# Reordering the start of a two-layer FFN kernel: conditioning products inside the first bank, one load issued by ScalarE, one product ahead of a mixing

## Chip, cores and metric

The kernel runs on one NeuronCore of a Trainium2 chip. The metric is the device time of one execution in microseconds (us); lower is better. Three executions of the kernel before gave a median of 1265.41 us (1264.41 to 1265.54).

## What is computed

The input `x` is 64 batches of 64 channels by 1024 values, in f32. Two layers follow each other, each a small conditioned mixing over channels, an expert FFN and a residual addition:

```python
x = x + _L0_ffn_ref(_L0_cond_ref(x, cond_128, ...), weight, lora_A, lora_B, gw1, ..., gw2, gb2)
x = x + _L1_ffn_ref(_L1_cond_ref(x, cond_128, ...), W, b, Wq, Wk, A, Bm)
# _L0_cond_ref: att = softmax(gelu(gelu(cond W0 + b0) W1 + b1) W2 + b2)   (64 x 8)
#               out = (sum_k att_k weight_k) x + att @ bias_k             (64 x 64 mixing per batch)
# _L0_ffn_ref:  out = x W^T + top-2 gated LoRA experts;  _L1_cond_ref: grouped convolution with 9 taps
```

The mixing over channels and the product with the FFN weights commute. The kernel therefore multiplies the unmixed `x` with the weights first, and mixes the result afterwards.

## The kernel before, in words

**Tiles and stages.** The 4096 rows (64 batches x 64 channels) are 32 tiles of 128. Phase A computes the first layer for all tiles and spills its result, phase B computes the second. Every f32 product is made as three products of a high and a low part (`split_product`, L1343 to L1347: hi x hi, hi x lo, lo x hi). So each weight piece and each tile of `x` is first rounded by ScalarE (ACT: `split_hi`, L724; `x_high`, L739), and VectorE (DVE) subtracts to get the low part (`split_lo`, L957; `x_low`, L979).

**Banks.** The first layer has 1184 output columns in three banks (k = 0, 1, 2 of 384, 416 and 384 columns). `main(t, b, k, j0, j1)` (L1409) is tile t's product with bank k over the pieces j0 to j1 of the contraction, 8 in all, three matmuls each. `mix(t, b, k)` (L1429) is the mixing of that bank, three matmuls. Between them ACT rounds the product (`y_high`, L746) and DVE makes its low part (`y_low`, L985). DVE builds the mixing matrix of a tile (`mix_matrix`, L962, about 2.3 us of small operations) and adds the mixed result into a row buffer (`evict`, L991). Tile t's bank 0 mixing writes one PSUM bank for all t, so `mix(2, 2, 0)` waits for `evict(1, 1, 0)`.

**The start.** TensorE (PE) begins with eight throw-away products of 512 columns (`keep_warm`, L1349) and then runs `first_bank` (L1390): tile 0's product with bank 0, piece by piece as the weights arrive, with the column sums of the weights woven in, five matmuls a piece. It needs the second half of tile 0's `x` (pieces 4 to 7) in high and low form for j = 4. The weights of bank 0 come as 8 chunks of 192 KB (n = 0 to 7); chunks 8 to 11 are the halves of banks 1 and 2. `column_sums(k)` (L1379) makes the sums for banks 1 and 2.

**Conditioning.** `cond(0)` to `cond(4)` (L1357) are the small products of the attention over kernels: two hidden layers with a Gelu on ACT after each (L796, L799), the logits, a softmax shared by ACT (L802, after an activation table load at L800) and DVE (L1045 to L1052), a masked product (L1054), then `cond(3)` (L1369), three products whose results give the coefficients `attc` (L1060), and `cond(4)`. No mixing matrix can be built without `attc`.

**Order.** All engines run hand-written orders; semaphores join them. Loads before the change are all issued by SyncE (SP), in program order, on one DMA queue. The orders that matter are SP's at L457 to L487, ACT's at L779 to L826, DVE's at L1025 to L1081 and PE's at L1447 to L1463. Then each engine enters `phase_a(t, b, it)`, whose first call is t = 0, through `periods` (L300). PE's `phase_a` is at L1465, ACT's at L828, DVE's at L1089.

Of the kernel before, what the change touches and what calls it, by code (L numbers as in the profile page):

```python
# [25 lines left out]
P = 128  # L26
# [46 lines left out]
def program(nc, a, out):  # L73
    with ExitStack() as ctx:
# [207 lines left out]
        def half_x(t, h):  # L282

            return xo[:, t, 512 * h:512 * h + 512].rearrange("p (j t) -> p j t", j=4)
# [142 lines left out]
        def _(sp):  # L427
            def chunk(n):
                for m in before[n]:
                    sp.wait_ge(*low_of(m))  # L430
                for src, to, _, _ in parts_of(n):
                    sp.dma_start(to, src).then_inc(stage_in[where[n]], 16)  # L432
# [22 lines left out]
                sp.dma_start(bias_in[:, u, :], src.unsqueeze(0).to_broadcast([P, P])).then_inc(bias_ld[u], 16)  # L455

            sp.dma_start(xo[:, 0, 0:512], a["xt"][0:P, 0:512]).then_inc(first_in, 16)  # L457
            for n in range(4):
                chunk(n)
            sp.dma_start(xo[:, 0, 512:D], a["xt"][0:P, 512:D]).then_inc(xt_in[0], 16)  # L460
            for n in range(4, 8):
                chunk(n)
            sp.dma_start(cbuf[:, 0:CPACK], a["cpack"]).then_inc(cond_in, 16)
            sp.dma_start(xo[:, 1, 0:512], a["xt"][P:2 * P, 0:512]).then_inc(second_in, 16)
# [258 lines left out]
        def _(act):  # L723
# [56 lines left out]
            act.activation(sc[:, 7:8], eps[:, :], ACT.Gelu).then_inc(tables, 1)  # L780
            act.wait_ge(first_in, 16)
            act.activation(x_hl[0][0][:, 0:4, :], half_x(0, 0), ACT.Copy).then_inc(first_hi, 1)
            for n in range(4):
                split_hi(n)
            act.wait_ge(xt_in[0], 16)
            act.activation(x_hl[0][0][:, 4:8, :], half_x(0, 1), ACT.Copy).then_inc(x_hi, 1)
            for n in range(4, 8):
                split_hi(n)
            act.wait_ge(second_in, 16)
            act.activation(x_hl[1][0][:, 0:4, :], half_x(1, 0), ACT.Copy).then_inc(first_hi, 1)  # L790
            act.wait_ge(xt_in[1], 16)
            act.activation(x_hl[1][0][:, 4:8, :], half_x(1, 1), ACT.Copy).then_inc(x_hi, 1)
            y_high(0, 0)
            act.wait_ge(cond_in, 16)
            act.wait_ge(cond_pe, 1)
            act.activation(h1, ps[:, BC[0], 0:B], ACT.Gelu, bias=cb0).then_inc(cond_act, 1)  # L796
            x_high(2, 2, 1)
            act.wait_ge(cond_pe, 2)
            act.activation(h2, ps[:, BC[1], 0:B], ACT.Gelu, bias=cb1).then_inc(cond_act, 1)  # L799
            act.activation(sc[:, 6:7], eps[:, :], ACT.Exp).then_inc(tables, 1)  # L800
            act.wait_ge(cond_dve, 2)
            act.activation(ex, lg, ACT.Exp, bias=am[:, 0:1]).then_inc(cond_act, 1)  # L802
            column_sums(0)
            split_hi(8)
            y_high(1, 0)
            split_hi(9)
            act.wait_ge(cond_pe, 7)
            for h in range(2):
                q = slice(64 * h, 64 * h + 64)
# [18 lines left out]
            def phase_a(t, b, it):  # L828
                if later(t, 2):
                    y_high(t + 2, 0)  # L830
                bias12_of(t + 1)
                if later(t, 1):
                    y_high(t, 1)
                    root(routed(t))
                y_high(t, 2)
                if before_end(t, XB):
                    x_high(t + XB, b, it + 2)
                if at(t, 0):
                    y_high(3, 0)
                    root(1)  # L840
                if before_end(t, AHEAD):
                    bias0_of(t + AHEAD)
                if isinstance(t, int) and t in aside:
                    split_hi(aside[t])
                if at(t, CATCH_UP):
                    root(t + 2)
# [95 lines left out]
        def _(dve):  # L942
# [91 lines left out]
            for n in range(4, 8):  # L1034
# [1 line left out]
            dve.wait_ge(first_hi, 2)  # L1036
            dve.tensor_tensor(x_hl[1][1][:, 0:4, :], half_x(1, 0), f32(x_hl[1][0][:, 0:4, :]),
                              ALU.subtract).then_inc(first_lo, 1)
            dve.wait_ge(x_hi, 2)
            dve.tensor_tensor(x_hl[1][1][:, 4:8, :], half_x(1, 1), f32(x_hl[1][0][:, 4:8, :]),  # L1040
                              ALU.subtract).then_inc(x_lo, 1)
            y_low(0, 0)
            x_low(2, 2)
            dve.wait_ge(cond_pe, 3)
            dve.tensor_tensor(lg, ps[0:B, BC[0], 64:64 + KATT], cb2, ALU.add).then_inc(cond_dve, 1)  # L1045
            dve.wait_ge(cond_dve, 1)
            dve.tensor_reduce(am[:, 0:1], lg, X, ALU.max, negate=True).then_inc(cond_dve, 1)
            dve.wait_ge(cond_act, 3)
            restart(0)
            link(dve.tensor_reduce(am[:, 1:2], ex, X, ALU.add))  # L1050
# [2 lines left out]
            dve.wait_ge(cond_dve, 3)  # L1053
            dve.tensor_tensor(att_m, att[:, None, :].to_broadcast([B, TILES, KATT]),  # L1054
                              batch_tile[:, :, None].to_broadcast([B, TILES, KATT]), ALU.mult).then_inc(cond_dve, 1)
            dve.wait_ge(cond_pe, 5)
            dve.tensor_copy(attT, ps[0:KATT, BC[1], 64:64 + B]).then_inc(cond_dve, 1)
            dve.tensor_tensor(ctxo, ps[0:B, BC[1], 128:128 + C], fs_bc, ALU.add).then_inc(cond_dve, 1)
            dve.wait_ge(cond_pe, 6)
            dve.tensor_copy(attc[:, :, :].rearrange("p t k -> p (t k)"),  # L1060
                            ps[:, BC[0], 128:128 + TILES * KATT]).then_inc(attc_ready, 1)
            split_lo(8)
            split_lo(9)
            dve.wait_ge(zeroed, 4)
            dve.wait_ge(consts_in, 16)
            dve.wait_ge(attc_ready, 1)
            restart(2)
            mix_matrix(0, 0)
            y_low(1, 0)
            split_lo(10)  # L1070
            mix_matrix(1, 1)
# [17 lines left out]
            def phase_a(t, b, it):  # L1089
                u = b % 2  # L1090
                restart(links_before(t))
                if later(t, 2):
                    if at(t, CATCH_UP + 1):
                        y_low(t + 2, 0)
                        evict(t - 1, 1 - u, 2)
                        x_low(t + XB - 1, (b + XB - 1) % XB)
                    else:
                        evict(t - 1, 1 - u, 2)
                        y_low(t + 2, 0)
                if at(t, 0):  # L1100
                    mix_matrix(3, 3)
                    y_low(0, 2)
                    evict(0, 0, 1)
                    evict(2, 0, 0)
                    x_low(4, 0)
                    y_low(3, 0)
                    evict(0, 0, 2)
                    route(1, 1)
                elif at(t, 1):
                    y_low(1, 1)  # L1110
                    route(2, 0)
                    y_low(1, 2)
                    evict(1, 1, 1)
                    evict(3, 1, 0)
                    mix_matrix(4, 0)
                    x_low(5, 1)
                else:
                    mix_matrix(t + AHEAD, (b + AHEAD) % XB)
                    y_low(t, 1)
                    evict(t + 2, u, 0)  # L1120
                    r = routed(t)
                    route(r, r % 2 if isinstance(t, int) else 1 - u)
                    y_low(t, 2)
                    evict(t, u, 1)
                    if at(t, CATCH_UP):
                        route(t + 2, u)
                    elif before_end(t, XB):
                        x_low(t + XB, b)
                assert at(t, CATCH_UP) or links["n"] == A_LINKS + at(t, 0), links["n"]
# [212 lines left out]
        def _(pe):  # L1342
# [47 lines left out]
            def first_bank():  # L1390

                (hi, lo), product, sums = x_hl[0], ps[:, BY0[0], 0:BANK0], ps[:, BM0[0], 0:BANK0]
                for j in range(J):
                    w_hi, w_lo, first, last = w0[0][:, j, 0, :], w0[0][:, j, 1, :], j == 0, j == J - 1
                    if j % 4 == 0:
                        pe.wait_ge(*((first_hi, 1) if first else (x_hi, 1)))
                    pe.wait_ge(stage_hi, j + 1)
                    pe.matmul(product, hi[:, j, :], w_hi, start=first, stop=False, skip_group_check=True)
                    pe.matmul(sums, ones[:, :], w_hi, start=first, stop=False, skip_group_check=True)
                    if j % 4 == 0:  # L1400
                        pe.wait_ge(*((first_lo, 1) if first else (x_lo, 1)))
                    pe.matmul(product, lo[:, j, :], w_hi, start=False, stop=False, skip_group_check=True)
                    pe.wait_ge(*low_of(j))
                    made = pe.matmul(product, hi[:, j, :], w_lo, start=False, stop=last, skip_group_check=True)
                    summed = pe.matmul(sums, ones[:, :], w_lo, start=False, stop=last, skip_group_check=True)
                made.then_inc(main_done[0], 1)
                summed.then_inc(wsum_done, 1)

# [39 lines left out]
            pe.wait_ge(wide_set, 1)  # L1448
            keep_warm(8)
            first_bank()  # L1450
            cond(0)
            main(1, 1, 0, 0, 2)
            cond(1)
            main(1, 1, 0, 2, 4)
            cond(2)
            main(1, 1, 0, 4, 8)
            cond(3)
            main(2, 2, 0, 0, 4)
            cond(4)
            main(2, 2, 0, 4, 8)  # L1460
            column_sums(1)
            pe.wait_ge(zeroed, 4)
            mix(0, 0, 0)  # L1463
# [1 line left out]
            def phase_a(t, b, it):  # L1465
                main(t, b, 1)
                if at(t, 0):
                    mix(1, 1, 0)
                    column_sums(2)
                mix(t + 2, (b + 2) % XB, 0)  # L1470
                main(t, b, 2)
                mix(t, b, 1)
                main(t + AHEAD, (b + AHEAD) % XB, 0)
                mix(t, b, 2)
# [218 lines left out]
```

## Time and profile before

| | before |
|---|---|
| profiled execution | 1265.09 us, span 1263.3 us |
| median of 3 (lowest, highest) | 1265.41 us (1264.41, 1265.54) |
| PE busy | 1257.2 us, 100% of the span, 6967 matmuls |
| DVE busy | 842.7 us, 67% |
| ACT busy | 307.3 us, 24% |
| POOL busy | 235.2 us, 19% |
| chain that ended last | PE 97%, DVE 1%, DMA 1% |

Read the table as follows: the span is what the profiler saw from the first instruction to the last, the execution's own time is 1.8 us longer. Matmuls are pipelined, and their ends are modelled; the distance from one start to the next shows PE's true pace, and a larger distance is time lost. The chain follows each piece of work back to what released it.

### The profile page before, as it was taken

What the parts mean: (1) busy time and instruction counts of PE and PEld (TensorE: products, weight loads), DVE (VectorE), ACT (ScalarE), POOL (GpSimd) and SP (SyncE); (2) the same over time, 40 slices, a digit from 0 to 9 for tenths busy, and PEclk for the clock granted to TensorE, in tenths of its full rate; (3) what the DMA queues carried; (4) which work ended last, traced back from release to release, by engine and by line L of the source; (5) the groups of instructions that cost most, each with busy time, mean ns of one, the idle gap of its engine ahead of it and who ended that gap; (6) DMA issues with size and microseconds to landing.
All of it is one profiled execution on the core that took longest, in us unless ns stands there. A gap on an engine that the chain in (4) does not pass through costs nothing.

```text
span 1263.3 us, 21216 instructions
## 1 busy us (share of the span) xinstructions
PE 1257.2 (100%) x6967; PEld 1165.1 (92%) x6967; DVE 842.7 (67%) x2171; ACT 307.3 (24%) x654; POOL 235.2 (19%) x170
## 2 busy tenths in 40 slices
PE   9999999999999999999999999999999999999998
PEld 8999999999999999888889889888888888988987
DVE  6877866667667667756765765675676576576563
ACT  6323332222223234211121121121121112112110
POOL 1244522232323222011001001001100100100100
PEclk9999999999999999999999999999999999999999
DMA  8355433333334267434223323322423322332310
GB/s 278 129 145 167 146 110 116 128 122 120 114 109 132 91 217 223 123 90 123 71 80 114 88 71 106 106 71 89 122 71 88 116 78 71 113 99 71 98 43 34
DMA packets 84889, 141.55 MB, mean 112 GB/s; under 512 B 6769, under 2 KB 53361, under 8 KB 84849
## 3 DMA queue, kind: packets, MB, share of 16 engines
q1 hardware_dynamic: 84848, 141.04, 36.7%
q8 instruction: 22, 0.36, 0.1%
q14 instruction: 19, 0.15, 0.0%
HBM read 88.57 MB, written 52.45 MB: 112 GB/s over the span
## 4 chain that ended last, share of the span: by engine, by line
PE 97%; DVE 1%; DMA 1%; ACT 0%; SPq 0%; issue 0%
PE ps L1345 30%; PE ps L1347 29%; PE ps L1346 29%; PE ps L1514 5%; PE ps L1516 2%; DMA xo<-in_xt 1%; DVE weights L960 1%; PE ps L1503 0%; PE ps L1480 0%; PE ps L1610 0%; DVE mixs L970 0%; PE ps L1505 0%; DVE mixw L969 0%; SPq L432 0%; ACT L800 0%
## 5 line engine op out<-in xcount | busy, mean ns | idle before, releaser
L1345 PE MATMUL ps<-weights,lhs_h 128*128 128x512 f32 (+3 forms) x1408 | 498.5, 354 | 0.0
L1347 PE MATMUL ps<-weights,lhs_l 128*128 128x512 f32 (+3 forms) x1408 | 489.1, 347 | 0.0
L1346 PE MATMUL ps<-weights,lhs_h 128*128 128x512 f32 (+3 forms) x1408 | 489.0, 347 | 0.0
L1345 PEld LDWEIGHTS ps<-weights,lhs_h 128*128 128x128 f32 x1408 | 264.5, 188 | 23.9 <-issue 0.6
L1347 PEld LDWEIGHTS ps<-weights,lhs_l 128*128 128x128 f32 x1408 | 264.5, 188 | 21.3
L1346 PEld LDWEIGHTS ps<-weights,lhs_h 128*128 128x128 f32 x1408 | 265.2, 188 | 19.8
L715 POOL TENSOR_TENSOR xo<-row,wsum 128x512 f32<-128x512 f32 x60 | 76.8, 1306 | 647.3 <-DMA out_x<-xo 647.3
L1345 PE MATMUL ps<-weights 128*128 128x384 f32 (+1 forms) x376 | 128.8, 343 | 0.0
L1346 PE MATMUL ps<-weights 128*128 128x384 f32 (+1 forms) x376 | 128.1, 341 | 0.0
L1347 PE MATMUL ps<-weights 128*128 128x384 f32 (+1 forms) x376 | 127.9, 340 | 0.0
L1231 DVE TENSOR_TENSOR whole<-ps,whole 64x256 f32<-64x256 f32 x240 | 101.2, 422 | 7.7
L752 ACT ACTIVATE part<-ps 128x384 fp32r<-128x384 f32 (+1 forms) x96 | 47.9, 499 | 239.9 <-PE ps L1347 239.9
L1224 DVE TENSOR_TENSOR whole<-ps,bias_in 64x256 f32<-64x256 f32 x240 | 101.1, 421 | 6.7 <-issue 0.2
L1514 PE MATMUL ps<-conv_hl,part 128*128 128x512 f32 x360 | 99.9, 345 | 0.0
L881 ACT ACTIVATE lhs_h<-whole 128x512 fp32r<-128x512 f32 x64 | 40.5, 633 | 235.6 <-DVE whole L1231 228.3
L988 DVE TENSOR_TENSOR part<-ps,part 128x384 fp32r<-128x384 f32 (+1 forms) x96 | 54.3, 565 | 61.0 <-ACT part L752 59.5
L668 POOL TENSOR_TENSOR row<-row,biased 128x800 f32<-128x800 f32 x31 | 61.2, 1974 | 127.3 <-DMA row<-in_xr 102.3
L1287 DVE TENSOR_TENSOR staging<-ps,mixw 128x256 f32<-128x256 f32 x32 | 13.6, 425 | 96.9 <-PE ps L1347 96.6
L1142 DVE TENSOR_TENSOR row<-ps,row 128x512 f32<-128x512 f32 x60 | 41.5, 692 | 52.8 <-PE ps L1347 52.5
L1514 PEld LDWEIGHTS ps<-conv_hl,part 128*128 128x128 f32 x360 | 67.7, 188 | 6.2
L1315 DVE TENSOR_TENSOR xo<-ps,xo 128x512 f32<-128x512 f32 x64 | 43.2, 692 | 45.3 <-PE ps L1347 45.1
L1347 PEld LDWEIGHTS ps<-weights 128*128 128x128 f32 x376 | 70.7, 188 | 0.4
(201 smaller groups left out, 1622.7 us busy)
## 6 DMA issues: line engine op xcount, KB each, us to landing
row<-spill SPq DMA_DIRECT2D x30, 576.0 KB, 4.2
z<-x_round SPq DMA_DIRECT2D x64, 256.0 KB, 5.1
out_x<-xo SPq DMA_DIRECT2D x31, 512.0 KB, 2.7
xo<-in_xt SPq DMA_DIRECT2D x30, 512.0 KB, 3.5
x_round<-row SPq DMA_DIRECT2D x60, 256.0 KB, 2.1
row<-in_xr SPq DMA_DIRECT2D x31, 400.0 KB, 3.2
spill<-row SPq DMA_DIRECT2D x31, 400.0 KB, 3.8
staging<-in_w SPq DMA_DIRECT2D x9, 832.0 KB, 6.1
```

The lines of the kernel that those rows point to most:

```text
L668: pool.tensor_tensor(dst, dst, biased[:, BANK0:OUT0], ALU.add).then_inc(row_ready12, 1)
L715: pool.tensor_tensor(natural[:, PAD * (1 - h):PAD * (1 - h) + J // 2, :], src[:, q].rearrange("p (s i) -> p s i", i=P), b1bc[:, q].rearran ...
L752: act.activation(yh[:, slot, 0:COLS0[k]], ps[:, BY0[slot], 0:COLS0[k]], ACT.Copy).then_inc(y_hi[k], 1)
L988: dve.tensor_tensor(yl[:, slot, 0:n], ps[:, BY0[slot], 0:n], f32(yh[:, slot, 0:n]), ALU.subtract).then_inc(y_lo[k], 1)
L1142: dve.tensor_tensor(base[:, q], ps[:, BP0[h], :], base[:, q], ALU.add).then_inc(x1_ready, 1)
L1224: dve.tensor_tensor(where_to[to, b], parts[q, :, k, 0], add[to, b, :, None, :].to_broadcast([64, 2, J, GC]), ALU.add).then_inc(conv_part, 1)
L1231: dve.tensor_tensor(where_to[to, b], parts[q, :, k, 1], where_to[to, b], ALU.add).then_inc(conv_read, 1)
L1315: dve.tensor_tensor(o, ps[:, BQ[2 + h], :], o, ALU.add).then_inc(y_read, 1)
L1345: pe.matmul(out_ap, lhs[0], rhs[0], start=first, stop=False, skip_group_check=True)
L1346: pe.matmul(out_ap, lhs[0], rhs[1], start=False, stop=False, skip_group_check=True)
L1347: return pe.matmul(out_ap, lhs[1], rhs[0], start=False, stop=last, skip_group_check=True)
L1514: pe.matmul(dst[:, out_k], stationary(t, 0, h, g, w), both[:, rows], start=(w == 1), stop=False, skip_group_check=True)
```

## The change

PE: `cond(0)` and `cond(1)` move into `first_bank`, behind its pieces j = 5 and j = 6; `cond(2)` follows `first_bank` at once; `cond(3)` and `cond(4)` stand later within the products of tiles 1 and 2. In `phase_a(0)`, `main(0, 0, 2)` goes in front of `mix(2, 2, 0)`. SP no longer issues the second half of tile 0's `x`; ACT issues it behind `split_hi(1)`, so SP's chunks 4 to 7 and all that follows go out one issue earlier. ACT and DVE serve the conditioning earlier among their other work. DVE builds mixing matrix 0 before splitting chunks 8 and 9, and `y_low(0, 0)` goes behind them. The same work is done in all: no matmul, no operation and no transfer is added or removed.

```diff
@@ SP
-            for n in range(4):
-                chunk(n)
-            sp.dma_start(xo[:, 0, 512:D], a["xt"][0:P, 512:D]).then_inc(xt_in[0], 16)
-            for n in range(4, 8):
+            for n in range(8):
                 chunk(n)
@@ ACT
-            for n in range(4):
+            for n in range(2):
+                split_hi(n)
+            act.dma_start(xo[:, 0, 512:D], a["xt"][0:P, 512:D]).then_inc(xt_in[0], 16)
+            for n in range(2, 4):
                 split_hi(n)
...
-            act.wait_ge(second_in, 16)
-            act.activation(x_hl[1][0][:, 0:4, :], half_x(1, 0), ACT.Copy).then_inc(first_hi, 1)
-            act.wait_ge(xt_in[1], 16)
-            act.activation(x_hl[1][0][:, 4:8, :], half_x(1, 1), ACT.Copy).then_inc(x_hi, 1)
-            y_high(0, 0)
             act.wait_ge(cond_in, 16)
             act.wait_ge(cond_pe, 1)
             act.activation(h1, ps[:, BC[0], 0:B], ACT.Gelu, bias=cb0).then_inc(cond_act, 1)
-            x_high(2, 2, 1)
+            act.wait_ge(second_in, 16)
+            act.activation(x_hl[1][0][:, 0:4, :], half_x(1, 0), ACT.Copy).then_inc(first_hi, 1)
             act.wait_ge(cond_pe, 2)
             act.activation(h2, ps[:, BC[1], 0:B], ACT.Gelu, bias=cb1).then_inc(cond_act, 1)
+            act.wait_ge(xt_in[1], 16)
+            act.activation(x_hl[1][0][:, 4:8, :], half_x(1, 1), ACT.Copy).then_inc(x_hi, 1)
             act.activation(sc[:, 6:7], eps[:, :], ACT.Exp).then_inc(tables, 1)
             act.wait_ge(cond_dve, 2)
             act.activation(ex, lg, ACT.Exp, bias=am[:, 0:1]).then_inc(cond_act, 1)
+            y_high(0, 0)
+            x_high(2, 2, 1)
             column_sums(0)
             split_hi(8)
+            split_hi(9)
             y_high(1, 0)
-            split_hi(9)
@@ ACT phase_a
+                if at(t, 0):
+                    y_high(0, 2)
                 bias12_of(t + 1)
                 if later(t, 1):
                     y_high(t, 1)
                     root(routed(t))
-                y_high(t, 2)
+                    y_high(t, 2)
@@ DVE
-            dve.wait_ge(x_hi, 2)
-            dve.tensor_tensor(x_hl[1][1][:, 4:8, :], half_x(1, 1), f32(x_hl[1][0][:, 4:8, :]),
-                              ALU.subtract).then_inc(x_lo, 1)
-            y_low(0, 0)
-            x_low(2, 2)
             dve.wait_ge(cond_pe, 3)
             dve.tensor_tensor(lg, ps[0:B, BC[0], 64:64 + KATT], cb2, ALU.add).then_inc(cond_dve, 1)
             dve.wait_ge(cond_dve, 1)
             dve.tensor_reduce(am[:, 0:1], lg, X, ALU.max, negate=True).then_inc(cond_dve, 1)
+            dve.wait_ge(x_hi, 2)
+            dve.tensor_tensor(x_hl[1][1][:, 4:8, :], half_x(1, 1), f32(x_hl[1][0][:, 4:8, :]),
+                              ALU.subtract).then_inc(x_lo, 1)
             dve.wait_ge(cond_act, 3)
...
+            x_low(2, 2)
             dve.wait_ge(cond_pe, 5)
...
-            split_lo(8)
-            split_lo(9)
...
             mix_matrix(0, 0)
+            split_lo(8)
+            split_lo(9)
+            y_low(0, 0)
             y_low(1, 0)
@@ DVE phase_a(0)
+                    y_low(0, 2)
                     mix_matrix(3, 3)
-                    y_low(0, 2)
@@ PE first_bank
+                    if j in (5, 6):
+                        cond(j - 5)
@@ PE
             first_bank()
-            cond(0)
-            main(1, 1, 0, 0, 2)
-            cond(1)
-            main(1, 1, 0, 2, 4)
             cond(2)
-            main(1, 1, 0, 4, 8)
+            main(1, 1, 0, 0, 4)
+            main(1, 1, 0, 4, 6)
             cond(3)
-            main(2, 2, 0, 0, 4)
+            main(1, 1, 0, 6, 8)
+            main(2, 2, 0, 0, 2)
             cond(4)
-            main(2, 2, 0, 4, 8)
+            main(2, 2, 0, 2, 8)
@@ PE phase_a
-                mix(t + 2, (b + 2) % XB, 0)
-                main(t, b, 2)
+                    main(0, 0, 2)
+                    mix(2, 2, 0)
+                else:
+                    mix(t + 2, (b + 2) % XB, 0)
+                    main(t, b, 2)
```

## Rows read from the trace of the kernel before

**Rows 1.** Waits of PE over the whole span: total us, times, longest

```profile
PE ps L1353 <- DVE weights L1025: 1.6, 1, 1.6
PE ps L1398 <- ACT weights L737: 0.7, 1, 0.7
PE ps L1371 <- DVE whole L1054: 0.3, 1, 0.3
PE ps L1345 <- DVE row L996: 0.2, 1, 0.2
```

**Rows 2.** Two stretches: us, busy (count) of PE, PEld, DVE, ACT, POOL, clock, DMA, GB/s

```profile
1.50:5.10 3.60, 3.55 (x8) 2.68 (x9) 0.96 (x2) 2.18 (x5) 0.41 (x2) 1.00 0.85 274
5.10:9.50 4.40, 3.69 (x21) 3.37 (x21) 2.35 (x5) 2.38 (x6) 0.00 (x0) 1.00 0.94 280
```

**Rows 3.** Timeline of PE: start us, length us, engine, line, operands, idle before

```profile
8.28 0.34 PE L1404 MATMUL ps<-weights 128*128 128x384 f32 x1
8.46 0.34 PE L1405 MATMUL ps<-weights,ones 128*128 128x384 f32 x1
9.53 0.41 PE L1398 MATMUL ps<-weights 128*128 128x384 f32 x1 [0.73 <-ACT weights L737]
...
15.76 0.34 PE L1347 MATMUL ps<-weights 128*128 128x384 f32 x1
16.03 0.28 PE L1367 MATMUL ps<-z 128*64 128x8 f32 x2
...
18.26 0.34 PE L1347 MATMUL ps<-weights 128*128 128x384 f32 x1
18.86 0.21 PE L1371 MATMUL ps<-consts,z 64*8 64x64 f32 x1 [0.27 <-DVE whole L1054]
...
24.75 3.22 PE L1386 MATMUL ps<-weights,ones 128*128 128x416 f32 x16
```

**Rows 4.** Chain that ended last, in order of time: start us, length us

```profile
3.09 5.22 DMA xo<-in_xt
```

**Rows 5.** Timeline of SP's DMA issues: start us, length us

```profile
3.58 1.86 SPq L432 DMA_DIRECT2D staging<-in_w  x4
5.48 0.43 SPq L463 DMA_DIRECT2D z<-in_cpack  x1
...
10.09 0.43 SPq L468 DMA_DIRECT2D consts<-in_consts  x1
```

**Rows 6.** DMA issues of x half 1, chunks 6 and 7, cpack, consts: KB, us to landing

```profile
xo<-in_xt SPq DMA_DIRECT2D x1, 256.0 KB, 2.7
staging<-in_w SPq DMA_DIRECT2D x2, 192.0 KB, 5.3
z<-in_cpack SPq DMA_DIRECT2D x1, 377.0 KB, 5.9
consts<-in_consts SPq DMA_DIRECT2D x1, 324.0 KB, 6.3
```

**Rows 7.** Timeline of ACT, same columns

```profile
4.27 1.02 ACT L737 ACTIVATE weights<-staging 128x384 fp32r<-128x384 f32 x2 [0.21 <-DMA staging<-in_w]
...
8.34 0.63 ACT L786 ACTIVATE weights<-xo 128x512 fp32r<-128x512 f32 x1 [1.28 <-DMA xo<-in_xt]
...
15.62 0.30 ACT L799 ACTIVATE z<-ps,z 128x64 f32<-128x64 f32 x1
15.94 1.28 ACT L800 ACT_TABLE_LOAD   x1
```

**Rows 8.** Timeline of DVE, same columns

```profile
18.30 0.42 DVE L1054 TENSOR_TENSOR whole<-z 64x256 f32<-64x256 f32 x1
...
20.34 3.69 DVE L960 TENSOR_TENSOR weights<-staging,weights 128x1664 fp32r<-128x1664 f32 x2
23.94 0.69 DVE L969 TENSOR_TENSOR mixw<-consts,attc 128x512 f32<-128x512 f32 x1
...
35.85 0.56 DVE L996 TENSOR_TENSOR row<-ps,row 128x384 f32<-128x384 f32 x1
```

## The prediction

> **What bounds the kernel now.** I read the waits of PE first. Over the whole span PE waits four times, 2.8 us in all [rows 1]: 1.6 us until its first instruction, 0.7 us in the first bank, 0.3 us in front of cond(3), 0.2 us in front of mix(2, 2, 0). Every other start follows from PE's own queue. The change adds and removes no work on PE, so it can give back at most what stands in these waits behind the first, plus the small bubbles around them. That is about 1.5 us of 1265. What it can lose has no such ceiling, since each moved wait stands in an in-order queue.
>
> The timeline of PE prices the waits, start to start. One 384-column matmul follows another after 0.18 us (8.28 to 8.46) [rows 3]. The first bank stands from 8.46 to 9.53, so 1.07 - 0.18 = 0.89 us are lost. Before cond(2), 16.03 - 15.76 - 0.17 = 0.10 us are lost, before cond(3) 18.86 - 18.26 - 0.17 = 0.43 us [rows 3]. The wait for the eviction is 0.20 us with 0.07 us for restarting the pipeline, my estimate from the longer first matmul after a wait (0.41 against 0.34 us) [rows 3].
>
> **Part 1, conditioning earlier.** cond(0) behind j = 5 would start when the five matmuls of j = 4 and of j = 5 are through. From the restart at 9.53 these ten take 10 x 0.175 = 1.75 us and the bubbles of j = 4 some 0.25 us more: 11.55 us. It needs cpack, issued at 5.48 and landed 5.9 us later, at 11.4 [rows 5, 6]: a cover of only 0.15 us. SP issues cpack one issue (0.47 us) sooner after the change, but the same bytes stand in front of it, so I leave its landing at 11.4.
> cond(1) needs h1. A small product takes about 0.3 us [rows 3], a Gelu 0.30 us, and from its end at 15.92 to cond(2) pass 0.11 us [rows 3, 7]. With 0.05 us to reach ACT that is 0.3 + 0.05 + 0.3 + 0.11 = 0.76 us, against 5 x 0.175 = 0.88 us of j = 6 that cover it. No wait. cond(2) needs h2, and ACT now has tile 1's first half (0.63 us, as a half in [rows 7]) between the two Gelus. h1 is done at about 12.25, that half at 12.9, cond(1) (12.7 + 0.3) at 13.05, h2 at 13.35, ready for PE at 13.5; PE comes there at 12.7 + 0.25 + 0.88 = 13.8. No wait, 0.3 us of cover. The 0.10 us before cond(2) goes. Behind it DVE has tile 1's first low half at about 13.6 for a product that starts at 14.1: no wait.
> cond(3): ACT rounds tile 1's second half (0.63 us) from 13.4 to 14.0 and then loads the Exp table. Before, from the start of that load (15.94) to cond(3) (18.86) passed 2.92 us [rows 3, 7], with DVE's att_m the last link (18.30 + 0.42) [rows 8]. So cond(3) could start at 14.0 + 2.9 = 16.9. PE comes there behind cond(2) and 18 matmuls, 13.8 + 0.3 + 18 x 0.175 = 17.25. The consts that its transpose needs land at 10.09 + 6.3 = 16.4 [rows 5, 6]. The 0.43 us goes, with 0.35 us of cover. Sum of this part: 0.53 us gained. If the cover fails somewhere, that part of 0.53 us comes back; below, the least this part gives is about 0.
>
> What comes late for it is x_low(2) on DVE, behind att_m: tile 2's high part is ready at about 17.2 (Exp at 15.5, then y_high(0, 0) and 1 us of x_high), the low part at 18.4; PE wants them at 17.25 + 1.1 + 6 x 0.175 = 19.4. No cost. SP waits for this low part before it issues chunk 10, some 1.4 us later than before; chunk 10 is not used before column_sums(2) at 32 us. No cost.
>
> **Part 2, DVE's order.** From 20.34 DVE works without a gap that matters until the eviction at 35.85 that releases mix(2, 2, 0) [rows 8]. Mixing matrix 0 now starts at about 19.2 instead of 23.94 and takes 2.3 us; the two splits (3.69 us) end at 25.0 instead of 24.0. PE's column_sums(1) used them from 24.75 [rows 3]; it will come at 24.2, and it needs the second chunk only after eight matmuls of 0.19 us, at 25.7. Cover 0.7 us, and chunk 8 itself is ready at 23.2. Then y_low(0, 0) ends at 25.5 for a mixing at 27.2. No cost, no gain in itself.
>
> **Part 3, main(0, 0, 2) in front of mix(2, 2, 0).** The eviction ends at 35.85 + 0.56 = 36.41, now about 35.6 since DVE starts its block some 1.2 us sooner and has y_low(0, 0) (0.5 us) added to it. PE would want it at 35.6 without this part; with 24 matmuls of 0.175 us (4.2 us) in front it wants it at 39.8. The wait of 0.20 + 0.07 us goes: 0.27 us gained, under 4 us of cover. main(0, 0, 2) needs chunk 11's low part (about 32.3) and y_low(2, 0) (about 32.8), both before 35.6. ACT's y_high(0, 2) and DVE's y_low(0, 2) are moved in step, 4 us ahead of mix(0, 0, 2). No cost.
>
> **Part 4, the second x half from ACT.** This is the part with an unknown price. Before, it was issued at 3.09 and landed 5.22 us later, at 8.31 [rows 4]; ACT took it up at 8.34 [rows 7], and PE restarted 1.2 us after that. ACT can issue it once chunk 1 has landed and split_hi(1) is handed over, between 4.8 and 5.3 us (the two splits run from 4.27 to 5.29) [rows 7]. Nothing in the trace shows a DMA on ACT, so the landing is bounded. Lower end: the first half took 2.7 us on an empty queue [rows 6], 4.8 + 2.7 = 7.5 us. Upper end: it queues behind all that SP has issued by then, as chunk 7 did, which was issued at about 5.0 and landed 5.3 us later at 10.3 [rows 5, 6] with the same bytes in front. Middle: it shares the engines half and half. Of the first half's 2.7 us, 256 KB at 274 GB/s are 0.96 us [rows 2], which leaves 1.75 us fixed; twice 256 KB at 280 GB/s are 1.87 us [rows 2]; 5.0 + 1.75 + 1.87 = 8.6 us. I take 8.6, nearest to what both the rows of the same size give. PE restarts 0.3 us later: 0.3 us lost. The ends are 0.5 to 0.7 us gained (then chunk 4 and cpack are next in the way) and 2.0 us lost.
> The Trainium skill ("DMA: Bandwidth & Descriptors", Queues, rings and completion order) says that each DMA engine goes round-robin between the queue rows that have work, packet by packet; by that rule the middle case would hold and the sum would be the one below. The same page (Issuing engines are not separate DMA queues) says that issuing from a second engine saves only the issuing time, which speaks against a gain from this part.
>
> **Sum.** 0.53 + 0.27 - 0.3 = 0.5 us gained. The profiled execution took 1265.09 us (span 1263.3), so 1264.6 us. The median of the three runs, 1265.41, lies 0.3 us above it, and the three differ by 1.1 us among themselves. The sum stands at 1264.6 to 1264.9; I give 1264.7. A measurement of this kernel can tell about 0.2%, 2.5 us, from no change, and no sum of these waits reaches that as a gain.
>
> **Rivals.**
> (a) Early landing, 7.5 to 8 us. For it: two queues feed the same engines, and the DMA engines are not full at every moment (0.94 busy) [rows 2]. Against: nothing in the trace shows a transfer overtaking others. Gain 0.8 + 0.6: 1263.7 us.
> (b) Late landing, about 10.3 us, behind everything SP has queued. For it: chunk 7's 5.3 us [rows 6]. PE would lose 2.0 us more in the first bank, the later chain shifts with it: 1265.1 - 0.8 + 2.0 = 1266.3 us.
> (c) Slower than before: late landing plus a fall of PE's clock. The place is j = 4 of the first bank. The eight opening products took 3.55 us, 444 ns each [rows 2], where 512 columns at the later pace are 0.175 x 512/384 = 0.23 us: they ran at the 1.2 GHz level although the clock column reads 1.00. The 0.73 us wait did not bring that level back, for the matmuls after it run at the full pace. A wait of 2.7 us might. One more stretch like the opening costs 3.55 - 8 x 0.23 = 1.7 us: 1268.0 us. It decides from a landing near 10 us on.
> The Trainium skill ("TensorE: Matmul & The Clock Gate", Part 1) says that the default is the slow clock and recent activity releases it; by that rule a long enough wait here would give (c), and the opening products agree with it.
> (d) The order does nothing: the conditioning chain is late all the same, because cpack lands after PE comes for it, or the half on ACT holds up h2. Then Part 1 gives 0 and cpack may cost up to 0.5 us: 1265.1 to 1265.6 us.
>
> **Chances.** Forecast 0.62, (a) 0.12, (b) 0.10, (c) 0.03, (d) 0.13. The range: 1263.5 covers most of (a), 1266.4 covers (b) and (d); left out are (c) and the edge of (a) and of run-to-run scatter. Faster by over 0.2% would take 2.5 us, more than all waits hold: 0.02. Slower by over 0.2% is (c) and an unseen cost of a second queue: 0.04. The rest, 0.94, is within 0.2%.
>
> **What would show it.** Right: PE's waits list no cond(3) and no eviction; only the opening wait and the one in the first bank remain, the latter 0.7 to 1.1 us; the half lands at 8.3 to 8.9; mixing matrix 0 starts near 19.2 us; column_sums(1) starts near 24.5, and the rest of the span is the same schedule 0.5 us earlier. Wrong: a wait of 2 us or more at j = 4, matmuls near 0.34 us start to start behind it, a wait in front of cond(0) on cpack, or any PE wait behind 40 us.

## The result

The changed kernel takes 1271.35 us (median of 5, 1269.92 to 1271.66) against 1265.41 us (1264.41 to 1265.92) for the kernel before: 1.0047 times as long, 95% interval 1.0033 to 1.006. It is 5.9 us slower, beyond the range, and on the side that I had given 4 in 100. The profiled execution took 1271.45 us, span 1269.7 us, 6.4 us more than before.

The waits of PE over the whole span, with the same columns as [rows 1]:

```profile
PE ps L1400 <- ACT weights L734: 3.4, 1, 3.4
PE ps L1355 <- DVE weights L1027: 1.6, 1, 1.6
PE ps L1347 <- DVE part L990: 1.1, 2, 0.8
```

The waits in front of cond(3) and of mix(2, 2, 0) are gone, as forecast. The wait in the first bank is 3.4 us instead of 0.7 us, and a new kind stands behind it: PE waits twice for y_low (L990). The timeline of PE at the first bank, to be laid beside [rows 3]:

```profile
5.10 0.52 PE L1400 MATMUL ps<-weights 128*128 128x384 f32 x1
5.42 0.52 PE L1401 MATMUL ps<-weights,ones 128*128 128x384 f32 x1
...
9.10 0.34 PE L1407 MATMUL ps<-weights,ones 128*128 128x384 f32 x1
12.80 0.42 PE L1400 MATMUL ps<-weights 128*128 128x384 f32 x1 [3.36 <-ACT weights L734]
...
14.30 0.52 PE L1400 MATMUL ps<-weights 128*128 128x384 f32 x1
14.62 0.52 PE L1401 MATMUL ps<-weights,ones 128*128 128x384 f32 x1
...
18.34 0.34 PE L1407 MATMUL ps<-weights,ones 128*128 128x384 f32 x1
...
50.02 0.34 PE L1347 MATMUL ps<-part,mix_hl 128*128 128x384 f32 x1
...
81.09 0.44 PE L1347 MATMUL ps<-part,mix_hl 128*128 128x384 f32 x1 [0.83 <-DVE part L990]
```

Start to start, j = 4 comes 3.70 us after the matmul in front of it; before it was 1.07 us. From 14.30 to 14.62 the matmuls stand 0.32 us apart, where 0.18 us is the full pace. The windows show the same, with the columns of [rows 2]: the granted clock is 0.58 in the stretch behind the wait.

```profile
9.50:12.80 3.30, 0.00 (x0) 0.03 (x1) 0.52 (x1) 1.19 (x3) 0.00 (x0) 1.00 0.46 178
12.80:16.90 4.10, 4.10 (x15) 3.86 (x15) 2.04 (x5) 1.48 (x5) 0.00 (x0) 0.58 0.71 236
```

The cause is in ACT's timeline and in the list of DMA issues (KB each, us to landing):

```profile
4.72 0.39 ACTq L782 DMA_DIRECT2D xo<-in_xt  x1
...
11.61 0.63 ACT L786 ACTIVATE weights<-xo 128x512 fp32r<-128x512 f32 x1 [4.94 <-DMA xo<-in_xt]
```

```profile
xo<-in_xt ACTq DMA_DIRECT2D x1, 256.0 KB, 6.9
```

ACT issued the half at 4.72 us, as early as I had assumed. It landed 6.9 us later, at 11.6 us. My three values were 7.5, 8.6 and 10.3 us.

Two rows of PE's timeline in the kernel before answer to the last two above:

```profile
46.11 0.41 PE L1345 MATMUL ps<-part,mix_hl 128*128 128x384 f32 x1
...
75.21 0.37 PE L1345 MATMUL ps<-part,mix_hl 128*128 128x384 f32 x1
```

**Where the 6.4 us come from.** The first matmul of mix(0, 0, 2) starts at 50.02 us here and at 46.11 us in the kernel before: 3.9 us later. That is made of 3.3 us for the late landing and 1.4 us for the low clock behind it, less the 0.8 us that the other parts gain. The first term is the distance of j = 4: ACT takes up the half at 11.61 instead of 8.34 us, and j = 4 starts 1.19 us behind that in both kernels, at 12.80 instead of 9.53 us. The gap on PE grew by 2.6 us only (3.70 against 1.07 us), because PE came to j = 4 0.6 us later: its clock rose later at the start (from 5.10 us to the last matmul of j = 3 it took 4.00 us, before 3.36 us). That cost nothing, since the half was not there. The second term: from 12.80 to 18.34 are 5.54 us, less 0.5 us for the two conditioning products; before, 9.53 to 13.14 were 3.61 us. The matmul at 81.09 us stands at 75.21 us in the kernel before, 5.9 us earlier: 2.0 us more are lost from 50 to 81 us. The rest of the 6.4 us, 0.4 us, comes near 500 us.

### The profile page after: what moved, and what is told of

Same layout as the page of the kernel before. It is cut to its first block, busy times and chain, and to the rows that moved or that the text cites. A ratio compares the mean times of both kernels' runs of the same rounds, so it can differ in the third digit from the quotient of the medians.

```text
span 1269.7 us, 21217 instructions
## 1 busy us (share of the span) xinstructions
PE 1260.2 (99%) x6967; PEld 1167.0 (92%) x6967; DVE 841.9 (66%) x2171; ACT 306.7 (24%) x654; POOL 234.9 (18%) x170
## 4 chain that ended last, share of the span: by engine, by line
PE 93%; DVE 4%; DMA 2%; issue 0%; POOL 0%; SPq 0%; ACT 0%; DVEq 0%; POOLq 0%
PE ps L1347 28%; PE ps L1349 28%; PE ps L1348 28%; PE ps L1519 5%; PE ps L1521 2%; DMA spill<-row 1%; DVE weights L962 1%; DMA xo<-in_xt 1%; DMA row<-spill 0%; PE ps L1508 0%; DVE row L998 0%; DVE mix_hl L975 0%; DVE part L990 0%; PE ps L1615 0%; PE ps L1485 0%
## 5 line engine op out<-in xcount | busy, mean ns | idle before, releaser
L990 DVE TENSOR_TENSOR part<-ps,part 128x384 fp32r<-128x384 f32 (+1 forms) x96 | 54.1, 565 | 60.9 <-ACT part L749 59.5
```

What stands on the lines that cost most here:

```text
L990: dve.tensor_tensor(yl[:, slot, 0:n], ps[:, BY0[slot], 0:n], f32(yh[:, slot, 0:n]), ALU.subtract).then_inc(y_lo[k], 1)
```

## The experiments

Each run was timed against the kernel before on the same chip: runs 1 to 4 on one chip (the kernel before took 1265.09 us there), runs 6 to 9 on a second (1265.24 us), runs 5 and 10 to 12 on a third (1265.39 us). The theory after the result: the second half lands late because it is on ACT's queue behind and beside SP's backlog, and the idle PE then falls to the low clock. The rivals: the moment of the issue alone is to blame; the new orders cost time by themselves.

**1. The half by SP again,** all other parts kept:

```diff
-            for n in range(8):
+            for n in range(4):
+                chunk(n)
+            sp.dma_start(xo[:, 0, 512:D], a["xt"][0:P, 512:D]).then_inc(xt_in[0], 16)
+            for n in range(4, 8):
                 chunk(n)
...
-            act.dma_start(xo[:, 0, 512:D], a["xt"][0:P, 512:D]).then_inc(xt_in[0], 16)
```

> The changed kernel with the second x half issued by SP again, between chunks 3 and 4; all other parts stay. If the half's late landing is the cause of the loss, it lands near 8.3 us, PE's wait in the first bank is 0.7 us, no stretch at half clock follows, and the time is my old sum without the half's term, 1264.3 to 1264.9 us. If the new orders of DVE and SP cost time by themselves (PE waited for y_low at 65 and 81 us, 1.9 us in all), those waits stay and it is 1266 to 1267 us. If nothing but the half's queue matters less than I think, it stays above 1268 us.

Measured: 1265.51 us (11 runs, 1264.39 to 1267.55), ratio 1.0001 (0.9992 to 1.001). So without the half's new place there is no slowdown. But the 0.8 us that I had summed for the other parts do not arrive either. Waits of PE in this run:

```profile
PE ps L1357 <- DVE weights L1029: 1.6, 1, 1.6
PE ps L1349 <- DVE part L992: 0.9, 1, 0.9
PE ps L1349 <- DVE mix_hl L1164: 0.3, 1, 0.3
```

There is no wait in the first bank, but that is luck of this execution: its clock rose late (matmuls 0.32 us apart until 7.7 us), so PE came to j = 4 only at 9.83 us, 0.3 us later than in the kernel before, and the half was there. Its mix(0, 0, 2) starts at 45.34 us, 0.77 us ahead of the kernel before. At 75.46 us the lead is gone, and PE is 0.25 us behind:

```profile
45.34 0.34 PE L1349 MATMUL ps<-part,mix_hl 128*128 128x384 f32 x1
...
75.46 0.44 PE L1349 MATMUL ps<-part,mix_hl 128*128 128x384 f32 x1 [0.92 <-DVE part L992]
```

**2. Only the half by ACT,** on the kernel before, with SP's and ACT's lines as in the change:

> The kernel before with this one part of the change: ACT issues the second x half behind the second piece. If the half is the cause, it lands near 11.6 us, PE waits 3.4 us in front of j = 4, a half-clock stretch of some 3.4 us follows, and the time is 1269.5 to 1271 us (the change without the 0.8 us that the other parts give). If the loss needs the new orders too, it is 1267 to 1269 us.

Measured: 1269.79 us (6 runs), ratio 1.0032 (1.002 to 1.0045). The time is within what was expected; its parts are not quite: in the profile the half took 6.1 us and was taken up at 11.08 us, sooner than I had expected, and the low clock lasted longer. The windows (columns as above) show the idle stretch and 5.8 us at half clock behind it:

```profile
8.50:12.30 3.80, 0.31 (x3) 0.06 (x1) 0.55 (x1) 1.22 (x3) 0.00 (x0) 0.87 0.71 270
12.30:18.10 5.80, 5.80 (x18) 5.80 (x19) 3.22 (x7) 2.10 (x5) 0.00 (x0) 0.50 0.77 267
```

PE is 4.8 us behind the kernel before at 51 us and still 4.8 us at 1250 us: nothing is added later. The profile of the changed kernel loses another 2 us from 50 to 81 us that this one does not, so the new orders matter once PE has been held up.

**3. The half by SP, late:** on SP's queue behind chunk 7, issued at 4.99 us, otherwise the change:

```diff
             for n in range(8):
                 chunk(n)
+            sp.dma_start(xo[:, 0, 512:D], a["xt"][0:P, 512:D]).then_inc(xt_in[0], 16)
```

> The changed kernel with the half issued by SP, at the same moment as ACT did but on SP's queue, behind chunk 7. If a transfer lands in the order of issue whatever queue it is on, it lands at 10.3 to 11 us and the time is 1269 to 1271 us, as with ACT. If ACT's queue is slow by itself (first packet 2.1 us after the issue, last packets late), it lands 1 us or more sooner than 11.6 us, and PE's wait is shorter by as much.

Measured: 1268.29 us (7 runs, 1266.28 to 1270.78), ratio 1.0029 (1.0017 to 1.004). In its profile, of an execution at 1266.28 us, the half took 4.5 us and landed at 9.5 us:

```profile
xo<-in_xt SPq DMA_DIRECT2D x1, 256.0 KB, 4.5
```

That is 2.1 us sooner than from ACT, although it was issued 0.27 us later. So the moment alone does not explain the landing. The executions scatter widely, and in most of them the mean clock of the span was 0.997 to 0.999 instead of 1.0: the shorter wait brings the low clock in some and not in others.

**4. The half by ACT, first of all:**

```diff
+            act.dma_start(xo[:, 0, 512:D], a["xt"][0:P, 512:D]).then_inc(xt_in[0], 16)
             act.wait_ge(zeroed, 2)
```

> The changed kernel with the half issued by ACT as its very first instruction, at about 0.7 us. If the moment of issue is what costs, the half lands by 4 to 5.5 us, the first half and the first chunks some 0.5 us later (their slack before PE starts at 5.1 us is 0.3 us), PE's wait in front of j = 4 is below 0.7 us, and the time is 1263.8 to 1265.5 us. If ACT's queue is slow by itself, the half still takes 6.9 us, lands at 7.6 us, and the time is the same within 0.5 us as with SP issuing it.

Measured: 1265.44 us (11 runs, 1264.32 to 1265.99), ratio 1.0 (0.9991 to 1.0009). The half took 3.3 us beside the first half's 3.4 us on SP's queue:

```profile
xo<-in_xt ACTq DMA_DIRECT2D x1, 256.0 KB, 3.3
xo<-in_xt SPq DMA_DIRECT2D x1, 256.0 KB, 3.4
```

ACT's queue is not slow by itself: the long landings, 6.1 to 6.9 us, are those that meet SP's backlog. The early issue has a price of its own, since the first half landed later: PE's first product of the first bank starts at 5.53 instead of 5.10 us.

**5. ACT's transfer with nothing issued behind it.** In the changed kernel SP holds back cpack and tile 1's halves until tile 0's second half has landed:

```diff
+            sp.wait_ge(xt_in[0], 16)
             sp.dma_start(cbuf[:, 0:CPACK], a["cpack"]).then_inc(cond_in, 16)
```

> The changed kernel, and SP issues cpack and tile 1's two halves only when the second half of tile 0 has landed, so that ACT's transfer meets only chunks 4 to 7 on SP's queue and nothing is issued behind it. If the transfers issued after it on SP's queue are what delays its last packets, it lands at 9 to 9.8 us instead of 11.6 us. If it waits only for what was issued before it, it stays at 11 us or later. The time itself says little here, since the conditioning data come 4 to 5 us later and PE waits for them in front of cond(0): 1271 to 1275 us.

Measured: the half was issued at 4.55 us and landed at 9.45 us. The chain that ended last has it as one piece:

```profile
4.55 4.90 DMA xo<-in_xt
```

So 2 us of the 6.9 us come from the three transfers that SP issues after it; against the 6.1 and 6.3 us of the same transfer in the profiles of runs 2 and 6 it is 1.2 and 1.4 us. The packets of the two queues (count, MB, share of the engines), in the changed kernel from 6.9 to 9 us and from 9 to 11.6 us, show how:

```profile
q1 hardware_dynamic: 241, 0.42, 61.9%
q10 hardware_dynamic: 123, 0.23, 35.2%
...
q1 hardware_dynamic: 352, 0.69, 68.6%
q10 hardware_dynamic: 19, 0.03, 3.7%
```

q10 is ACT's queue, q1 SP's. Of the 144 packets of the half, 2 start before 6.9 us, 123 within the next 2.1 us, and 19 trickle until 11.2 us, among 352 packets of SP's queue. The half counts as landed only behind the last. The Trainium skill ("DMA: Bandwidth & Descriptors", Queues, rings and completion order) says that an engine goes round-robin between queues; the trace agrees for the middle stretch in that both queues move packets there, though with two packets of SP's for one of ACT's. The first packet comes about 1.9 us after the issue; for such a start my half-and-half estimate had its fixed 1.75 us. What it lacked is the tail behind 9 us. The time, 1267.59 us (8 runs, ratio 1.0017, 1.0007 to 1.0027), was lower than I expected: cpack, issued 4.5 us later, landed at 12.5 us, before PE came to cond(0) at 12.7 us, and PE has no wait for it. In three of the eight executions the mean clock was 0.998 or 0.999, and these were the three fastest; the mean clock of a span alone does not say what the clock cost.

**6. The wait filled with work,** in the changed kernel:

```diff
+                    if j == 4:
+                        keep_warm(14)
                     if j % 4 == 0:
```

> The changed kernel with fourteen throw-away products of 512 columns (3.2 us) in the place where PE waits for the second x half, so that PE does not stand idle. If the idle stretch is what brings the 1.2 GHz level, it does not appear, the matmuls of j = 4 and 5 follow each other after 0.18 us, and the time is 1.5 to 2 us below the changed kernel's: 1269.3 to 1269.9 us. If the low clock has nothing to do with the idle stretch, the time stays at 1271.3 us.

Measured: 1268.70 us (6 runs, 1267.22 to 1270.91), ratio 1.003 (1.0018 to 1.0043), 2.65 us below the changed kernel, which was timed apart from it. The timeline of PE:

```profile
8.83 3.44 PE L1355 MATMUL ps<-weights,ones 128*128 128x512 f32 x14
12.18 0.41 PE L1402 MATMUL ps<-weights 128*128 128x384 f32 x1
...
13.33 0.34 PE L1402 MATMUL ps<-weights 128*128 128x384 f32 x1
13.50 0.34 PE L1403 MATMUL ps<-weights,ones 128*128 128x384 f32 x1
```

Behind a stretch as long as the wait, but busy, the matmuls follow each other after 0.17 us. So the idle PE is what brought the low clock in the profile; in one of the six executions the mean clock was still 0.999, so filling the wait is no full protection. By the two profiles the clock gives back the 1.4 us, and another 0.6 us is the landing: the half took 6.3 us here and 6.9 us there, and j = 4 starts at 12.18 instead of 12.80 us. What is lost behind 46 us differs too (0.3 against 2.4 us), so the 2.65 us are not the price of the clock alone. The Trainium skill ("TensorE: Matmul & The Clock Gate", Part 1) has the rule, recent activity releases the slow clock; this pair of runs agrees.

**7. Where the 0.8 us go, first theory: POOL's row.** In run 1 DVE stands 0.82 us in front of evict(2, 0, 0), whose row comes by a load behind a spill that SP issues late. Here SP issues the first two spills sooner:

```diff
+            for u in range(2):
+                sp.wait_ge(mix_read[0], u + 1)
+                spill0(u, u)
             sp.wait_ge(x_lo, 4)
             load_xt(5, 1)
             sp.wait_ge(cond_out, 16)
             load_bias(0, 0)
             load_bias(1, 1)
-            for u in range(2):
-                sp.wait_ge(mix_read[0], u + 1)
-                spill0(u, u)
```

> The run with the half by SP, and in SP's queue the two first spills moved ahead of the load of tile 5 and of the two bias loads, so that the row load behind the spill can start about 0.8 us sooner. Theory: PE's lead of 0.8 us at 46 us is given back at 75 us because DVE stands still from 46.1 to 46.9 us for POOL's row, and has no gap behind it until 80 us. Then that DVE wait falls below 0.2 us, PE's wait at 75 us falls from 0.9 to 0.3 us or less, and the time is 1264.2 to 1264.8 us. Rival: DVE is simply full of work from 20 to 80 us and POOL's row is not what matters; then PE's wait at 75 us stays, and the time is 1265.3 to 1265.6 us.

Measured: 1264.76 us (11 runs, 1263.98 to 1266.14), ratio 0.9996 (0.9987 to 1.0005). The wait of DVE for POOL's row is gone from the profile, yet PE still waits 0.8 us at 75 us. But DVE did not come any sooner: the two operations in front of its evictions now run beside POOL's add of the row (45.67 to 46.69 us) and take 1.29 us together, where they took 0.47 us in run 1. The timeline of DVE:

```profile
45.48 1.29 DVE L980 TENSOR_TENSOR mix_hl<-mixs,mix_hl 64x64 fp32r<-64x64 f32 x2
```

So this run did not take the 0.8 us from DVE, and it could not decide between the theory and its rival. The median is lower than run 1's, but within the scatter, and the profile is of the slowest execution (1266.14 us).

**8. The same on the kernel before:**

> The kernel before with only the two first spills moved ahead of tile 5's load and the bias loads. In the kernel before DVE waits only 0.17 us for POOL's row at 46.7 us, so both theories expect no more than 0.2 us: 1264.9 to 1265.3 us. A gain of 0.5 us or more would mean that the row's lateness cost the kernel before as well.

Measured: 1265.21 us (11 runs), ratio 0.9999 (0.999 to 1.0008). Nothing, as expected.

**9. The half between chunks 2 and 3,** on run 7's kernel:

> As the run with the spills first, and SP issues the second x half between chunks 2 and 3 instead of 3 and 4. The half should land 0.5 us sooner, at 7.8 us, chunk 3 0.6 us later, at 7.1 us, still before PE comes for it at 7.8 us. If PE's start is bound by the half, the wait at j = 4 shrinks by 0.4 to 0.5 us and the time is 1263.8 to 1264.3 us. If the later chunks are then late, or DVE binds at 75 us, it stays within 0.2 us of the run with the spills first.

Measured: 1264.83 us (11 runs, 1263.99 to 1266.03), ratio 0.9997 (0.9988 to 1.0006), the same as run 7. Its profile, of an execution at 1263.99 us, is the clue. It has no wait at 75 us and none in the first bank. What differs is POOL's add beside DVE's small operations. The timelines of POOL and DVE in run 1:

```profile
72.66 1.93 POOL L668 TENSOR_TENSOR row<-row,biased 128x800 f32<-128x800 f32 x1 [3.20 <-DMA row<-in_xr]
```

```profile
72.67 1.93 DVE L1022 TENSOR_TENSOR dv_all<-top 128x1 f32<-128x1 f32 x1
74.64 0.18 DVE L1023 TENSOR_TENSOR count<-count,oh_all 128x16 f32<-128x16 f32 x1
74.85 0.56 DVE L992 TENSOR_TENSOR part<-ps,part 128x384 fp32r<-128x384 f32 x1
```

An operation of one column takes 1.93 us, exactly as long as POOL's add that began 0.01 us before it, and y_low stands behind it. In run 9 the same add began at 72.25 us, after the last operation of the routing had started. The kernel before has the collision too: its timeline of DVE shows

```profile
72.70 1.79 DVE L1019 TENSOR_TENSOR count<-count,oh_all 128x16 f32<-128x16 f32 x1
74.53 0.56 DVE L988 TENSOR_TENSOR part<-ps,part 128x384 fp32r<-128x384 f32 x1
```

Its y_low ends at 75.09 us, and PE's matmul starts at 75.21 us: no wait, and no slack. So run 9's gain at 75 us is luck of the timing: its add began 0.4 us sooner than in run 1.

**10. POOL behind the routing,** on run 1's kernel:

```diff
                 if before_end(t, 4):
                     mix_product(t + 4)
+                if at(t, 2):
+                    pool.wait_ge(counted, 4)
                 row_init12(t + 1, 1 - u, it + u)
```

> The run with the half by SP, and POOL's phase of tile 2 waits until DVE has finished the routing of tile 3, so that POOL's add of 128x800 does not start while DVE is in the small operations of that routing. In the run with the half by SP a 128x1 operation of DVE took 1.93 us beside that add, and PE then waited 0.9 us for y_low. Theory: this meeting of POOL and DVE is where the lead of 0.8 us is given back; then no small DVE operation near 72 us takes over 0.3 us, PE does not wait at 75 us, and the time is 1264.3 to 1264.8 us. Rival: DVE is late by its own amount of work and the slow operation only stands where it would wait anyway; then PE's wait stays near 0.9 us and the time near 1265.5 us.

Measured: 1264.43 us (11 runs, 1263.58 to 1265.36), ratio 0.9991 (0.9982 to 1.0), 1.0 us below the kernel before; run 1, on its own chip, was 0.4 us above it. Timelines of POOL and DVE:

```profile
73.44 1.96 POOL L668 TENSOR_TENSOR row<-row,biased 128x800 f32<-128x800 f32 x1 [3.66 <-DVE count L1025]
```

```profile
73.40 0.56 DVE L994 TENSOR_TENSOR part<-ps,part 128x384 fp32r<-128x384 f32 x1
73.87 0.58 DVE L1002 TENSOR_TENSOR row<-ps,row 128x416 f32<-128x416 f32 x1
74.37 2.11 DVE L988 TENSOR_TENSOR lhs_l<-xo,lhs_h 128x1024 fp32r<-128x1024 f32 x1
```

y_low starts 1.45 us sooner, PE does not wait for it, and the add now delays x_low (2.11 us instead of 1.22), which nobody waits for. The profile does lose elsewhere: DVE waits 1.22 us for POOL's row, as its timeline shows,

```profile
47.57 0.56 DVE L1002 TENSOR_TENSOR row<-ps,row 128x384 f32<-128x384 f32 x1 [1.22 <-POOL row L658]
```

and PE's lead over the kernel before shrinks from 1.20 us at 50 us to 0.45 us at 60 us. So the row that run 7 was after does cost PE something when it is late enough; 0.82 us of it in run 1 cost nothing. y_low and the eviction, which read PSUM, keep their 0.56 and 0.58 us beside the add. The Trainium skill ("SBUF — State Buffer", Who interferes with whom) says that GpSimd and a DVE operation with two SBUF inputs hold one port pair exclusively and that the second to start blocks; these rows agree: x_low, with two SBUF inputs, ends 1.08 us behind the add, the operations that read PSUM are not held.

**11. The same on the kernel before:**

> The kernel before with POOL's wait alone. There PE does not wait at 75 us, since y_low ends at 75.1 us and PE comes for it at 75.4 us, so nothing can be gained: 1265.0 to 1265.4 us. Slower by 0.5 us or more would mean that POOL's later adds hold up evictions.

Measured: 1265.40 us (11 runs), ratio 1.0 (0.9991 to 1.0009). PE had nothing to gain there, and gains nothing. (PE comes for y_low at 75.21 us, not at 75.4 us as I had written.)

**12. Everything that helped together:** the half between chunks 2 and 3, the spills first, POOL behind the routing:

> The half by SP between chunks 2 and 3, the first spills first, and POOL behind the routing of tile 3. If the meeting at 72 us is all that takes the lead away, the lead of 1.1 us that the run with the earlier half had at 46 us is kept in every execution: 1263.9 to 1264.4 us, and the spread narrows. If it is not, 1264.8 us as without POOL's wait.

Measured: 1264.37 us (11 runs, 1263.85 to 1264.77) against 1265.39 us (33 runs, up to 1266.98), ratio 0.9992 (0.9983 to 1.0001). Only the opening wait is left on PE, and its 11 executions spread over 0.9 us:

```profile
PE ps L1359 <- DVE weights L1031: 1.6, 1, 1.6
```

Its lead of 1.1 us at 46 us is kept to the end of the span, so in this profile neither the loss of run 1 near 75 us nor that of run 10 before 60 us stands. Its median is the lowest, though only 0.06 us below run 10's, which is no difference. The gain of 1.0 us is as large as its uncertainty.

## Why the prediction was wrong

**Parts 1 to 3 were right to 46 us.** The three waits went, no new one stands among cond(0) to cond(4), mixing matrix 0 starts at 19.20 us in run 1 where I had said 19.2, and run 1 leads by 0.77 us where I had summed 0.80 us. That this is so near is partly luck: j = 4 started 0.3 us late there, and the rest gained 1.1 us. In the profiles of runs 3, 7, 9, 10 and 12 PE gains 0.9 us from j = 4 to 46 us.

**The step that failed first is Part 4's landing.** I bounded it by 7.5 and 10.3 us and took 8.6; it was 11.6 us. The upper bound took chunk 7, which has the same bytes in front of it on one queue. It left out that transfers issued afterwards on the other queue pass between the half's packets: run 5 shows that these cost 1.2 to 2 us, and without them the half landed at 9.45 us, inside my bounds. The late landing cost 3.3 us at j = 4 instead of the 0.3 us of my sum.

**The clock was named and mis-weighted.** Rival (c) had the mechanism, the place and the side: a long wait at j = 4, then the half clock. It was priced at 1268.0 us, with 2.0 us for the wait and 1.7 us for the clock, and given 3 in 100. The profile shows 3.3 us and 1.4 us. Run 2, which has the wait and the clock without the other parts, gives 1269.8 us; its profile has 2.7 us for the landing and 2.4 us for a longer stretch at the low clock, so the price of the clock was mis-sized too, and it differs from execution to execution. I had tied (c) to a landing at 10.3 us, and gave that little because the range of the landing was too narrow.

**The other step that failed is the sentence that every other start follows from PE's own queue.** It is true as a reading of [rows 1], and wrong as a statement about slack. DVE's y_low at 75 us was 0.1 us ahead of PE. A lead of PE therefore ends there in run 1; the profiles of runs 3, 4, 5 and 7 lose 0.9 to 1.0 us at the same matmul, beside POOL's add, those of runs 2, 6, 9, 10 and 12 nothing. The held-up schedule of the changed kernel loses 2.0 us from 50 to 81 us. Laid beside the kernel before, its PE loses 0.4 us by 60 us, after DVE has waited 1.06 us for POOL's row, 0.5 us at 65.48 us, after an operation of 16 columns took 0.88 us beside POOL's row operation, and 1.1 us at 81.09 us, after one took 1.82 us beside POOL's add. Timelines of POOL and DVE:

```profile
63.38 1.02 POOL L655 TENSOR_TENSOR row<-row,biased 128x384 f32<-128x384 f32 x1 [6.94 <-DMA row<-in_xr]
...
78.50 1.91 POOL L665 TENSOR_TENSOR row<-row,biased 128x800 f32<-128x800 f32 x1 [3.28 <-DMA row<-in_xr]
```

```profile
52.42 0.56 DVE L998 TENSOR_TENSOR row<-ps,row 128x384 f32<-128x384 f32 x1 [1.06 <-POOL row L655]
...
63.55 0.88 DVE L1018 TENSOR_TENSOR oh_all<-consts,idf 128x16 f32<-128x16 f32 x1
...
78.63 1.82 DVE L1021 TENSOR_TENSOR count<-count,oh_all 128x16 f32<-128x16 f32 x1
```

So three quarters of it are meetings of POOL and DVE. That is read from one profile; no run removed them from the changed kernel itself. The late row waits for a spill which SP issues behind two bias loads, in the queue that I had passed over as "no cost".

**Open:** the last 0.4 us near 500 us. PE waits there for the result of DVE's `tw_low`, a low part in phase B (0.3 us in run 1's profile, 0.5 us in run 7's), in some profiles and not in others; nothing was tried on it. The time at which the clock rises at the start also differs, from about 5 us in run 2's profile to 7.7 us in run 1's; I have not tried what sets it. And in how many executions the low clock came at the first bank is known only from mean clocks.

## What to carry to other kernels

A missing wait in a profile says that nothing is late, not by how much. Before a lead is booked, look up for each hand-over behind it how early the other engine was, at least until that engine has idle time of its own.

In this kernel the transfer that was moved to a second queue was delayed by what was issued after it as well as by what stood before it. If the bound engine waits for it, issue it before the backlog (run 4) or keep it in the queue's order (run 1), and count the clock with the wait.

## What I had not expected

The same 256 KB took 3.3 us on ACT's queue at 0.7 us, 4.9 us at 4.55 us with nothing behind it, 6.9 us at 4.72 us with 0.9 MB issued behind it (6.1 and 6.3 us in the profiles of two other runs), and 4.5 us on SP's queue at 4.99 us. And a DVE operation of 128x1 elements took 1.93 us instead of 0.16 us, because a POOL add of 128x800 had begun 0.01 us before it; at that place run 1's profile loses 1.1 us of the whole kernel.
